# Cross attention's softmax by blocks of 1024 keys instead of by two passes over all keys

## The chip, the cores and the metric

The kernel runs on one core of one Trainium2 chip. The metric is the device time of one execution in microseconds (us), lower is better. Five engines work from queues of their own: TensorE (PE in the profile; PEld are its weight loads), VectorE (DVE), ScalarE (ACT), GpSimd (POOL) and SyncE (SP), which issues most DMAs. Each runs its instructions in the order of its queue, and they wait for each other by semaphores.

## The reference

The whole program is a decoder of six parts over 1024 tokens of width 128 and a context of 6404 rows of width 96. The change is in the second part, single-head cross attention (all in float32):

```python
def _L0_xattn_ref(query, key, value, Wq, bq, Wk, bk, Wv, bv):
    q = jnp.einsum('bqd,dh->bqh', query, Wq) + bq      # query: layernorm of x, 1024 x 128
    k = jnp.einsum('bkd,dh->bkh', key, Wk) + bk        # key and value: ctx_768, 6404 x 96
    v = jnp.einsum('bkd,dh->bkh', value, Wv) + bv
    scores = jnp.einsum('bqh,bkh->bqk', q, k)
    weights = jax.nn.softmax(scores, axis=-1)
    return jnp.einsum('bqk,bkh->bqh', weights, v)      # added to x
```

The kernel never makes k or v. It multiplies the queries by the key weights (`qc`, 97 x 1024: 96 context columns and one for the bias), takes scores as `qc` against the context, sums the context's rows by the weights, and applies the value weights to that sum (`w_v`). A column of ones in the context (`ctx_rows`, 97 columns) gives the softmax's denominator.

## The kernel before

Each engine's queue in a part is written out by hand; what stands behind a wait on an engine waits too. `cross_attention` works in two passes, with PSUM's eight banks of 128 x 512 as its workspace.

The **first pass** goes over 8 tiles of 128 queries, and for each over 7 chunks of 1024 keys (the last has 260). PE makes the scores of a chunk, 128 queries by 1024 keys, with two matmuls of 512 columns (L1001), into one of three pairs of banks; DVE takes the maximum over the keys (L957). The scores are then lost. At every eighth chunk a unit of another piece of work is laid in, the keys of a later part ("film keys"): PE multiplies (L800), ACT rounds to bf16 (`hi`, L819; `mid`, L813), DVE and POOL take the remainders (`rest`, L829; `low`, L844), SP stores. There are 7 units of 1024 keys.

Between the passes the maxima are put into the queries, so that the second pass's scores come out with the maximum subtracted (L1007, L1009, L1065).

The **second pass** goes over 51 tiles of 128 keys (the last has 4). PE makes the scores again, now with keys on the partitions and all 1024 queries as columns (L1033, two matmuls), ACT takes the exponential (L1078, 128 x 1024), and PE sums the context's rows by these weights into two banks (L1018, two matmuls with the 97 context columns as weights). Beside it runs a third piece of work, the convolution kernel of a later state-space part ("s4d"): 16 groups, for each of which DVE makes angles (L546, L632, L634, L635), POOL decays (L653), ACT sines and exponentials (L680, L684), DVE their product (L619), PE a product (L715), and for each two groups ACT copies and PE turns the rows (L692, L727, L699). ACT does a pair of groups as one step: a table load and two sines, a table load and two exponentials.

At the end DVE copies the sum out of PSUM (L967) and PE applies the value weights (L1043), eight small matmuls between DVE's divisions (L971, L972).

Every float32 product of PE is two instructions in the profile; a transpose is one.

## Time and profile before

| | us |
|---|---|
| runs of the kernel before | 1661.75, 1729.4, 1659.3; median 1661.75 |
| the profiled execution: its own time | 1659.78 |
| the profiled execution: its span | 1657.9 |
| cross attention's first pass starts, its second pass ends, in the span | 191.7, 504.0 |
| mean granted clock of TensorE over the span | 0.933 of 2.4 GHz |

The span is the profiled time from the first to the last instruction; the remaining 1.9 us lie around it. Times given as places are counted from the span's start. Matmuls are pipelined: a row's length runs to the modelled end of its last instruction, so the pace of a stream of them is the distance between starts.

### The profile page before, as it was taken

What the parts mean: (1) busy time and instruction counts of PE and PEld (TensorE: products, weight loads), DVE (VectorE), ACT (ScalarE), POOL (GpSimd) and SP (SyncE); (2) the same over time, 40 slices, a digit from 0 to 9 for tenths busy, and PEclk for the clock granted to TensorE, in tenths of its full rate; (3) what the DMA queues carried; (4) which work ended last, traced back from release to release, by engine and by line L of the source; (5) the groups of instructions that cost most, each with busy time, mean ns of one, the idle gap of its engine ahead of it and who ended that gap; (6) DMA issues with size and microseconds to landing.
All of it is one profiled execution on the core that took longest, in us unless ns stands there. A gap on an engine that the chain in (4) does not pass through costs nothing. (4 is left out here: it accounts for less than half of the span.)

```text
span 1657.9 us, 19830 instructions
## 1 busy us (share of the span) xinstructions
PE 1369.8 (83%) x6709; PEld 729.4 (44%) x6763; DVE 1255.7 (76%) x2833; ACT 897.2 (54%) x1424; POOL 678.3 (41%) x466
## 2 busy tenths in 40 slices
PE   6677699999997757889899988989875459999798
PEld 2223344333344434355555555555564323333465
DVE  5999567866515669999999999999878657776433
ACT  4666211457543320687778778877852146666311
POOL 2656111112101034688787878878861120000012
PEclk9799899999997878999999999999987759999899
DMA  6000011000005832000000000000040300000000
GB/s 152 1 0 1 28 58 49 0 1 0 1 0 125 174 103 63 1 1 1 1 1 1 1 1 1 1 1 1 7 152 1 89 1 1 1 1 1 1 0 14
DMA packets 32482, 42.99 MB, mean 26 GB/s; under 512 B 14286, under 2 KB 25644, under 8 KB 30992
## 3 DMA queue, kind: packets, MB, share of 16 engines
q1 hardware_dynamic: 29820, 29.61, 6.2%
q10 hardware_dynamic: 2552, 12.02, 3.5%
q8 instruction: 56, 0.92, 0.2%
q14 instruction: 54, 0.44, 0.1%
HBM read 33.48 MB, written 8.14 MB: 25 GB/s over the span
## 5 line engine op out<-in xcount | busy, mean ns | idle before, releaser
L1631 PE MATMUL psum<-film_ka,film_context_qa 97*128 97x427 bf16 (+3 forms) x896 | 329.8, 368 | 74.3 <-DVE film_stage_kept L1810 29.4
L2033 ACT ACTIVATE film_stage_e<-psum,film_stage_bias 128x512 f32<-128x512 f32 (+1 forms) x416 | 273.9, 668 | 96.9 <-PE psum L1633 87.0
L1810 DVE MAX8 film_stage_kept<-psum 128x8 f32<-128x213 f32 (+1 forms) x960 | 318.5, 377 | 6.6 <-PE psum L1633 6.3
L1633 PE MATMUL psum<-film_kb,film_context_qb 128*128 128x427 bf16 (+2 forms) x843 | 306.4, 364 | 0.0
L1882 POOL TENSOR_TENSOR film_stage_e<-film_stage_e 128x1024 f32<-128x1024 f32 (+1 forms) x91 | 207.1, 2276 | 80.7 <-DVE film_stage_e L1852 60.8
L1852 DVE SCALAR_TENSOR_TENSOR film_stage_e<-psum,film_context_top,film_stage_e 128x512 f32<-128x512 f32 (+1 forms) x325 | 231.8, 719 | 8.4 <-ACT film_stage_e L2033 6.7
L1631 PEld LDWEIGHTS psum<-film_ka,film_context_qa 97*128 97x128 bf16 x896 | 92.1, 103 | 195.3 <-DVE film_stage_kept L1810 86.8
L3235 POOL TENSOR_TENSOR residual<-residual,top_expert_kept 128x1024 f32<-128x1024 f32 x7 | 16.5, 2351 | 294.9 <-DVE top_expert_kept L3192 294.9
L1913 PEld LDWEIGHTS psum<-ctx_rows,film_stage_mean_T 128*128 128x128 f32 (+1 forms) x816 | 121.9, 192 | 30.0 <-issue 3.3
L2998 DVE TENSOR_REDUCE gqa_attend_low<-psum 128x1 f32<-128x128 f32 (+7 forms) x128 | 94.1, 755 | 43.1 <-PE psum L2917 40.7
L1913 PE MATMUL psum<-ctx_rows,film_stage_mean_T 128*128 128x96 f32 (+1 forms) x816 | 119.9, 269 | 1.8
L1872 POOL TENSOR_TENSOR film_stage_e<-film_stage_e,film_stage_keep 128x512 f32<-128x512 f32 (+1 forms) x91 | 102.1, 1122 | 32.7 <-ACT film_stage_keep L2009 32.4
L1885 POOL TENSOR_TENSOR film_stage_mean<-film_stage_e 128x512 f32<-128x512 f32 (+1 forms) x91 | 111.8, 1229 | 7.1
L3035 ACT ACTIVATE gqa_attend_prob<-psum 128x512 f32<-128x512 f32 x192 | 84.9, 486 | 51.4 <-PE psum L2930 50.6
L1018 PE MATMUL psum<-cross_attention_prob,ctx_rows 128*97 128x512 f32 (+1 forms) x204 | 99.7, 612 | 12.4 <-ACT cross_attention_prob L1078 12.4
L342 POOL TENSOR_TENSOR mamba_drive<-mamba_relu,mamba_b_all 128x1024 f32<-128x1024 f32 x32 | 77.2, 2414 | 64.7 <-ACT mamba_b_all L467 34.6
L1633 PEld LDWEIGHTS psum<-film_kb,film_context_qb 128*128 128x128 bf16 x896 | 89.7, 100 | 30.4 <-issue 3.6
L1078 ACT ACTIVATE cross_attention_prob<-psum 128x1024 f32<-128x1024 f32 (+1 forms) x51 | 51.0, 1018 | 87.0 <-PE psum L1033 87.0
L1033 PE MATMUL psum<-oss_attention_qc_shifted,ctx_T 97*128 97x512 f32 (+1 forms) x204 | 97.4, 600 | 0.8 <-ACT oss_attention_qc_shifted L1065 0.8
L957 DVE TENSOR_REDUCE cross_attention_tops<-psum 128x1 f32<-128x1024 f32 (+1 forms) x56 | 61.3, 1109 | 36.6 <-PE psum L1001 36.5
L1001 PE MATMUL psum<-ctx_T,cross_attention_qc 97*128 97x512 f32 (+1 forms) x208 | 87.3, 576 | 0.7 <-issue 0.7
L1897 PE MATMUL psum<-ident,film_stage_mean 128*128 128x128 f32 (+1 forms) x408 | 78.4, 273 | 6.1 <-ACT film_stage_mean_T L1985 5.0
(548 smaller groups left out, 2540.3 us busy)
## 6 DMA issues: line engine op xcount, KB each, us to landing
film_kb<-film_k_rows ACTq DMA_DIRECT2D x4, 1601.0 KB
film_ka<-film_k_rows ACTq DMA_DIRECT2D x3, 1601.0 KB
ctx_T<-in_ctx_T SPq DMA_DIRECT2D x1, 2401.5 KB
gqa_experts_w<-in_L_ffn_W SPq DMA_DIRECT2D x1, 2048.0 KB
film_stage_e<-in_dft_ahead SPq DMA_DIRECT2D x1, 1728.0 KB, 8.7
film_k_rows<-cross_attention_film_hi SPq DMA_DIRECT2D x6, 256.0 KB, 2.0
film_k_rows<-cross_attention_film_mid SPq DMA_DIRECT2D x6, 256.0 KB, 2.0
film_k_rows<-cross_attention_film_low SPq DMA_DIRECT2D x6, 256.0 KB, 2.0
```

The costliest lines, as they stand in the source:

```text
L1018: last = pe.matmul(ps[0:CA, 6 + n, :], ctx[0:rows, k, :], prob[0:rows, k % 3, n * HALF:(n + 1) * HALF], start=k == 0, stop=k == KT - 1)
L1033: last = pe.matmul(ps[0:rows, 2 * (k % 2) + n, :], ctx_T[:, k * P:k * P + rows], qc_shifted[:, n * HALF:(n + 1) * HALF], start=True, stop= ...
L1631: pe.matmul(out, a["qa"][0:ROWS, h, rows], a["ka"][0:ROWS, h, c + b:c + b + cols], start=True, stop=False)
L1633: last = pe.matmul(out, a["qb"][:, h, rows], a["kb"][:, h, c + b:c + b + cols], start=False, stop=True)
L1810: last = dve.max(kept[:, h % 2, PER_PIECE * u + s, :], bank[:, lo:hi])
L1852: dve.scalar_tensor_tensor(out=w, in0=weigh_bank(n, h), scalar=a["top"][:, NH * i + h, TOP - 1:TOP], in1=w, op0=ALU.is_ge, op1=ALU.mult).t ...
L1872: link(pool.tensor_tensor(w[h], w[h], keep[:, k % KEEPS, 0:width], ALU.mult))
L1882: link(pool.tensor_tensor(pairs[:, :, 0, :], pairs[:, :, 0, :], pairs[:, :, 1, :], ALU.add))
L1885: pool.tensor_tensor(out, w[0], w[2], ALU.add).then_inc(mean_ready, 1)
L1913: last = pe.matmul(ps[:, 7, 0:DC], mean_T[0:r, n % 2, b:b + P], ctx[0:r, (c + b) // P, 0:DC], start=c + b == 0, stop=c + b + r == S2)
L2033: act.activation(e[:, n % RING, sub, 0:PIECES[u][1]], ps[:, SEARCH_BANKS + q % WEIGH_BANKS, 0:PIECES[u][1]], ACT.Exp, bias=bias[:, i % 2, ...
L2998: dve.tensor_reduce(low[:, b, i:i + 1], pair(2 * (step % 2), (i + 1) * P), AX, ALU.max, negate=True).then_inc(max_read, 1)
```

## The change

The two passes become one loop over 56 blocks (8 query tiles by 7 chunks of up to 1024 keys), with n as the count of the loop:

- PE makes the scores of block n once (L1092 of the changed kernel), queries on the partitions, from queries of opposite sign. DVE takes the minimum over the block's keys (`shift`), and ACT the exponential against that block's own extreme (L1158).
- PE turns the weights of block n-2 with the identity, 128 keys at a time (`turn`, L1049), into PSUM; ACT copies them to SBUF, 512 columns at a time (`copy_turned`, L1129 and L1132); PE multiplies the turned weights (now the stationary operand, 128 x 128) with the 97 columns of the context (`weighted`, L1062). 408 transposes and 408 products in all.
- The sums of the 7 blocks of a query tile stand side by side in one bank, the first four and then the last three. DVE copies them out (`copy_part`), ACT makes the factors between the blocks' extremes (`scale`), and POOL multiplies and adds them (`bring_together`, four instructions for a tile). At the end PE turns the eight sums and ACT copies them (L1177).
- Scores now have two pairs of banks instead of three; two banks are for turned weights, one for the sums, and one (`side`) for the other two pieces of work.
- The film keys come in 13 units of 512 keys, one a block from n = 1. The s4d work is spread by tables over the blocks from n = 2 to 59. A pair's two sines and two exponentials now stand in two successive blocks.
- SP loads the film mask and the s4d inputs ahead of the value weights; POOL's `memset` of `minus_top` is gone; DVE clears the side bank first.

On PE, in the loop. Before, a stretch of the second pass (L1033 scores, L1018 weighted sums):

```order
L1018 MATMUL psum<-cross_attention_prob,ctx_rows 97x512 x2
L1033 MATMUL psum<-cross_attention_qc_shifted,ctx_T 128x512 x2
L1018 MATMUL psum<-cross_attention_prob,ctx_rows 97x512 x2
L1033 MATMUL psum<-cross_attention_qc_shifted,ctx_T 128x512 x2
L1018 MATMUL psum<-cross_attention_prob,ctx_rows 97x512 x2
```

Now, one block of the loop and the start of the next:

```order
L1049 MATMUL psum<-ident,cross_attention_prob 128x128 x4
L1062 MATMUL psum<-ctx_rows,cross_attention_prob_T 128x97 x4
L1092 MATMUL psum<-ctx_T,cross_attention_qc 128x512 x2
L1049 MATMUL psum<-ident,cross_attention_prob 128x128 x4
L1062 MATMUL psum<-ctx_rows,cross_attention_prob_T 128x97 x4
L735 MATMUL psum<-ident,cross_attention_s4d_rows 128x128 x4
L1049 MATMUL psum<-ident,cross_attention_prob 128x128 x4
```

A block's transposes and products stand in halves around the scores of the block two later; an s4d turn (L735) or product stands at a block's end.

On ACT, around one s4d step. Before, in the second pass:

```order
L692 ACTIVATE cross_attention_s4d_rows<-psum 128x512
L680 ACT_TABLE_LOAD
L680 ACTIVATE cross_attention_s4d_i_angle<-cross_attention_s4d_i_angle 128x1024 x2
L684 ACT_TABLE_LOAD
L684 ACTIVATE cross_attention_s4d_i_decay<-cross_attention_s4d_i_decay 128x1024 x2
L1078 ACTIVATE cross_attention_prob<-psum 128x1024 x2
```

Now:

```order
L1129 ACTIVATE cross_attention_prob_T<-psum 128x512 x2
L1158 ACTIVATE cross_attention_prob<-psum,cross_attention_shift 128x1024
L689 ACT_TABLE_LOAD
L689 ACTIVATE cross_attention_s4d_i_angle<-cross_attention_s4d_i_angle 128x1024 x2
L1129 ACTIVATE cross_attention_prob_T<-psum 128x512 x2
L1158 ACT_TABLE_LOAD
L1158 ACTIVATE cross_attention_prob<-psum,cross_attention_shift 128x1024
L695 ACTIVATE cross_attention_s4d_i_decay<-cross_attention_s4d_i_decay 128x1024 x2
L1129 ACTIVATE cross_attention_prob_T<-psum 128x512 x2
```

Two copies of turned weights now precede each exponential, and the sines (L689) and the decays' exponentials (L695) stand ahead of the copies of the next block.

The core of the diff (the s4d and film functions are cut into steps by index, with the same instructions; the s4d steps are called as shown):

```diff
 def s4d_scalar(act, k, step):
...
-    else:
-        q = 2 * (step - 3)
+    elif step % 2:
+        q = step - 3
         for b in range(2):
             act.wait_ge(sem["i_ready"], q + b + 1)
             angle = k["i_angle"][:, (q + b) % RING_Q]
             act.activation(angle, angle, ACT.Sin, scale=TURN).then_inc(sem["sin_done"], 1)
+    else:
+        q = step - 4
         for b in range(2):
             act.wait_ge(sem["grown"], q + b + 1)
...
+S4D_SMALL_AT = {0: 2, 1: 3, 6: 4, 7: 5, 8: 6, 2: 7, 3: 8, 4: 9, 5: 10, 9: 11, 10: 12}
+S4D_FROM = 12
...
-KEY_PARTS, KEY_RESTS, KEYS_FIRST, KEYS_EVERY = 2, 2, 4, 8
+KEY_UNITS = [(c, min(HALF, S2 - c)) for c in range(0, S2, HALF)]
+KEY_PARTS, KEY_RESTS, KEYS_FIRST = 2, 2, 1
...
+    LAG, PROBS, TURNED = 2, 3, 3
+    FIRST_PART = 4
+    key_at = {KEYS_FIRST + u: u for u in range(len(KEY_UNITS))}
+    small_at = {n: part for part, n in S4D_SMALL_AT.items()}
+    angles_at = {S4D_FROM + 5 * x // 4: divmod(x, 2) for x in range(2 * NG)}
+    pair_at = [S4D_FROM + 5 * p for p in range(NG // 2)]
+    scalar_at = {5: 1, 8: 2}
+    for p, n in enumerate(pair_at):
+        scalar_at[n + 4], scalar_at[n + 5] = 2 * p + 3, 2 * p + 4
+    decay_at = {n + 2 * b: 2 * p + b for p, n in enumerate(pair_at) for b in range(2)}
+    power_at = {n + 6 + b: 2 * p + b for p, n in enumerate(pair_at) for b in range(2)}
+    product_at = {n + 8 + b: 2 * p + b for p, n in enumerate(pair_at) for b in range(2)}
+    rows_at = {n + 10: p for p, n in enumerate(pair_at)}
+    turn_at = {n + 11: p for p, n in enumerate(pair_at)}
+    kernel_at = {n + 12: p for p, n in enumerate(pair_at)}
...
+            def bring_together(i):
+                pool.wait_ge(part_copied, 2 * i + 2)
+                pool.wait_ge(scale_ready, i + 1)
+                x = sums[:, i % 2]
+                link(pool.tensor_tensor(x, x, scale[:, i, :].unsqueeze(2).to_broadcast([P, NB, CA]), ALU.mult))
+                link(pool.tensor_tensor(x[:, 0:3], x[:, 0:3], x[:, 3:6], ALU.add))
+                link(pool.tensor_tensor(x[:, 0:2], x[:, 0:2], x[:, 2:7:4], ALU.add))
+                pool.tensor_tensor(total[:, i, :], x[:, 0], x[:, 1], ALU.add).then_inc(total_ready, 1)
...
         @block.vector
         def _(dve):
...
+            for n in range(END):
+                if n in parts_at:
+                    copy_part(parts_at[n])
+                if n < BLOCKS:
+                    i, c = divmod(n, NB)
                     dve.wait_ge(score_done, n + 1)
+                    dve.tensor_reduce(shift[:, i, c:c + 1], scores(n), AX, ALU.min).then_inc(shift_ready, 1)
...
+                if n in key_at:
+                    film_key_vector(dve, film, side, key_at[n])
+                if n in small_at:
+                    s4d_vector_small(dve, link, s4d, side, small_at[n])
+                if n in angles_at:
+                    s4d_vector_angles(dve, link, s4d, *angles_at[n])
+                if n in power_at:
+                    s4d_vector_power(dve, s4d, power_at[n])
...
         @block.tensor
         def _(pe):
+            def turn(n, h):
+                k = half_at[n, h]
+                pe.wait_ge(prob_ready, n + 1)
+                if k >= 2:
+                    pe.wait_ge(turned, k - 1)
+                for _, x, rows in key_tiles(n, h):
+                    last = pe.transpose(ps[0:rows, 4 + k % 2, x:x + P],
+                                        prob[:, n % PROBS, h * HALF + x:h * HALF + x + rows], g["ident"][:])
+                last.then_inc(turn_done, 1)
+            def weighted(n, h):
+                k = half_at[n, h]
...
+                pe.wait_ge(turned, k + 1)
+                if h == 0 and c in (0, FIRST_PART) and part >= 1:
+                    pe.wait_ge(part_copied, part)
+                for tile, x, rows in key_tiles(n, h):
+                    last = pe.matmul(ps[:, SUMS_BANK, place:place + CA], prob_T[0:rows, k % TURNED, x:x + P],
+                                     ctx[0:rows, tile, :], start=tile % 8 == 0,
+                                     stop=tile == min(8 * c + 7, KT - 1))
...
+            for n in range(END):
+                b = n - LAG
+                if 0 <= b < BLOCKS:
+                    turn(b, 0)
+                if 0 <= b - 1 < BLOCKS:
+                    weighted(*HALVES[half_at[b - 1, 0] + ((b - 1, 1) in half_at)])
+                if n < BLOCKS:
+                    if n >= 2:
+                        pe.wait_ge(prob_ready, n - 1)
...
+                if (b, 1) in half_at:
+                    turn(b, 1)
+                    weighted(b, 0)
+                if n in key_at:
...
+                    film_key_tensor(pe, film, ctx_T, side, key_at[n])
+                if n in product_at:
...
+                    s4d_tensor(pe, s4d, side, product_at[n])
+                if n in turn_at:
+                    s4d_turn(pe, s4d, side, turn_at[n])
...
         @block.scalar
         def _(act):
...
+            for n in range(END):
+                b = n - LAG
+                for h in range(2):
+                    if (b, h) in half_at:
+                        copy_turned(b, h)
+                if n < BLOCKS:
+                    act.wait_ge(shift_ready, n + 1)
+                    act.activation(prob[:, n % PROBS, 0:width(n)], scores(n), ACT.Exp, scale=-1.0,
+                                   bias=shift[:, i, c:c + 1]).then_inc(prob_ready, 1)
...
+                if n in key_at:
+                    film_key_high(act, film, side, key_at[n])
+                if n - 1 in key_at:
+                    film_key_middle(act, film, key_at[n - 1])
+                if n in scalar_at:
+                    s4d_scalar(act, s4d, scalar_at[n])
+                if n in rows_at:
+                    s4d_copy_rows(act, s4d, side, rows_at[n])
+                if n in kernel_at:
+                    s4d_copy_kernel(act, s4d, side, kernel_at[n])
```

## Rows read from the trace of the kernel before

**Rows 1.** Busy time by stretch; columns: stretch, its length, engines, PEclk, DMA

```profile
191.00:290.00 99.00, 96.91 (x234) 44.30 (x234) 68.22 (x64) 15.48 (x17) 13.42 (x7) 1.00 0.14 50
295.00:504.00 209.00, 196.46 (x696) 78.56 (x695) 110.58 (x125) 116.84 (x123) 27.99 (x15) 0.98 0.00 1
```

**Rows 2.** Instructions of two lines of PE: ns min/median/max, first and last start

```profile
L1001 PE MATMUL psum<-ctx_T,cross_attention_qc x208: 381/592/667, 191.7 to 288.3; 97*128 97x512 f32 x96, 97*128 97x260 f32 x8
...
L1018 PE MATMUL psum<-cross_attention_prob,ctx_rows x204: 587/592/1071, 298.3 to 503.3; 128*97 128x512 f32 x100, 4*97 4x512 f32 x2
```

**Rows 3.** Timeline of PE in both passes: start, us to the last end

```profile
255.81 12.62 PE L1001 MATMUL psum<-ctx_T,cross_attention_qc 97*128 97x512 f32 x30
...
376.68 0.62 PE L715 MATMUL psum<-ss_attention_s4d_i_angle,cross_attention_s4d_left 128*8 128x128 f32 x16
377.23 0.66 PE L727 MATMUL psum<-ident,cross_attention_s4d_rows 128*128 128x128 f32 x4
377.73 1.88 PE L1033 MATMUL psum<-oss_attention_qc_shifted,ctx_T 97*128 97x512 f32 x4
```

**Rows 4.** Timeline of PE in causal attention and film context, later parts

```profile
571.34 1.95 PE L1376 MATMUL psum<-causal_attention_v,causal_attention_pT 128*128 128x128 f32 x16
573.13 0.82 PE L1364 MATMUL psum<-ident,causal_attention_score 128*128 128x128 f32 x6
573.78 1.02 PE L1351 MATMUL psum<-causal_attention_kT,causal_attention_qT 128*128 128x512 f32 x2
...
901.36 0.58 PE L1913 MATMUL psum<-ctx_rows,film_stage_mean_T 128*128 128x96 f32 x4
901.78 0.35 PE L1631 MATMUL psum<-film_ka,film_context_qa 97*128 97x426 bf16 x1
```

**Rows 5.** Weight loads of L1376: ns min/median/max, first and last start

```profile
L1376 PEld LDWEIGHTS psum<-causal_attention_v,causal_attention_pT x72: 186/192/192, 571.2 to 589.9; 128*128 128x128 f32 x72
```

**Rows 6.** The stretch of causal attention's stream, columns as in Rows 1

```profile
570.00:580.00 10.00, 8.41 (x61) 7.03 (x60) 6.23 (x15) 4.13 (x8) 0.00 (x0) 1.00 0.42 86
```

**Rows 7.** Timeline of ACT around one s4d step of the second pass

```profile
337.65 1.02 ACT L1078 ACTIVATE cross_attention_prob<-psum 128x1024 f32<-128x1024 f32 x1 [2.41 <-PE psum L1033]
338.69 1.28 ACT L680 ACT_TABLE_LOAD   x1
339.99 2.00 ACT L680 ACTIVATE ss_attention_s4d_i_angle<-ss_attention_s4d_i_angle 128x1024 f32<-128x1024 f32 x2
...
345.21 1.92 ACT L1078 ACTIVATE cross_attention_prob<-psum 128x1024 f32<-128x1024 f32 x2
```

**Rows 8.** PE after that step: timeline, its stretch, and waits in 295 to 504

```profile
342.61 1.88 PE L1033 MATMUL psum<-oss_attention_qc_shifted,ctx_T 97*128 97x512 f32 x4
346.27 3.63 PE L1018 MATMUL psum<-cross_attention_prob,ctx_rows 128*97 128x512 f32 x4 [1.78 <-ACT cross_attention_prob L1078]
...
346.00:350.00 4.00, 3.73 (x5) 1.47 (x6) 3.90 (x4) 1.13 (x2) 2.58 (x1) 0.57 0.02 4
...
PE psum L1018 <- ACT cross_attention_prob L1078: 12.4, 9, 2.8
```

**Rows 9.** Durations on ACT, DVE and POOL: ns min/median/max; the last by form

```profile
L1065 ACT ACTIVATE oss_attention_qc_shifted<-psum x2: 597/597/597, 292.3 to 294.1; 97x512 f32<-97x512 f32 x2
...
L2033 ACT ACTIVATE film_stage_e<-psum,film_stage_bias x416: 459/687/707, 669.6 to 1222.4; 128x512 f32<-128x512 f32 x128, 128x260 f32<-128x260 f32 x11
...
L957 DVE TENSOR_REDUCE cross_attention_tops<-psum x56: 418/1224/1226, 193.8 to 289.4; 128x1 f32<-128x1024 f32 x48, 128x1 f32<-128x260 f32 x8
...
L1885 POOL TENSOR_TENSOR film_stage_mean<-film_stage_e 128x512 f32<-128x512 f32 x84 | 106.7, 1270 | 6.6
```

**Rows 10.** Timeline at the start of cross attention and at its end

```profile
177.55 7.39 DVE L100 TENSOR_SCALAR cross_attention_xn<-residual,cross_attention_mv,cross_attention_rstd 128x128 f32<-128x128 f32 x8
...
179.12 5.67 POOL L836 TENSOR_SCALAR s_attention_film_masking<-ross_attention_film_mask 4x1601 bf16<-4x1601 uint8 x1 [3.49 <-DMA ross_attention_film_mask<-in_vision_mask]
...
505.28 0.71 PE L1043 MATMUL psum<-cross_attention_w_v,cross_attention_summed_c 97*128 97x129 f32 x4 [1.39 <-DVE cross_attention_summed_c L967]
```

More of the change, by code:

```diff
@@ L623, in s4d_vector, with s4d_vector_angles @@
+def s4d_vector_angles(dve, link, k, q, part):
+    sem = k["sem"]
+    b = q % RING_Q
+    group = slice(q * GROUP, (q + 1) * GROUP)
     i_index = k["index"][:, 0:P].unsqueeze(1).to_broadcast([P, GROUP, P])
[L624 to L626 removed]
+    if part == 0:
         if q >= RING_Q:
@@ new lines, in weighted @@
+            def weighted(n, h):
+                k = half_at[n, h]
+                i, c = divmod(n, NB)
+                part = 2 * i + (c >= FIRST_PART)
+                place = (c - part_blocks(part)[0]) * CA
+                pe.wait_ge(turned, k + 1)
[5 more added lines that the diff above has]
+                                     stop=tile == min(8 * c + 7, KT - 1))
+                if (n, h + 1) not in half_at and c in (FIRST_PART - 1, NB - 1):
+                    last.then_inc(part_done, 1)
@@ L1047, in _, with copy_turned @@
         def _(act):
+            def copy_turned(n, h):
+                k = half_at[n, h]
+                act.wait_ge(turn_done, k + 1)
+                whole = sum(rows == P for _, _, rows in key_tiles(n, h)) * P
+                last = act.activation(prob_T[:, k % TURNED, 0:whole], ps[:, 4 + k % 2, 0:whole], ACT.Copy)
+                for _, x, rows in key_tiles(n, h):
+                    if rows < P:
+                        last = act.activation(prob_T[0:rows, k % TURNED, x:x + P], ps[0:rows, 4 + k % 2, x:x + P],
+                                              ACT.Copy)
+                last.then_inc(turned, 1)
             root(act, rstd, 1, var_ready, root_ready)
```

455 lines of the change are left out of this document (213 added, 242 removed).

## The prediction

> **What bounds the kernel now.** I read the busy time by stretch first, because the change lies in cross attention alone. PE is busy for 96.9 of 99 us in the first pass and 196.5 of 209 us in the second, while no other engine passes 117 us [rows 1]. So PE bounds both passes. Then I read places: the scores begin at 191.7 and the last weighted sum starts at 503.3 [rows 2], and the value weights follow at 505.3 [rows 10]. The stretch from 191.7 to 505.3 is 313.6 us; this is what the change replaces. Last I read PE's pace, the distance between starts, since a row's length holds a pipelined end. The question is what PE has to do in the new loop, and whether DVE and ACT, which now stand inside one chain with it, let it do so.
>
> **PE's work, before and after.** 30 score instructions of 512 columns take 12.62 us [rows 3], less the last one's overhang of 0.16, so 0.43 us each; a product is two, 0.86. One 1024-key block of scores costs 1.72. The second making of the scores and the wide sums (each 51 x 2 products, some 88 us at this pace) go. In their place stand 408 transposes and 408 products of 97 columns with fresh 128-column weights. The trace has both kinds in later parts. Six transposes take 573.78 - 573.13 = 0.65 us, 0.11 each; 16 product instructions of 128 columns take 573.13 - 571.34 = 1.79, 0.112 each; four of 96 columns take 0.42, 0.105 each [rows 4]. The nearest bounds are thus 0.105 and 0.112 for a product instruction (I take 0.107, since 97 columns is next to 96) and 0.11 to 0.125 for a transpose, the upper from four s4d transposes between 377.23 and 377.73 [rows 3]; I take 0.11, the longer stream.
>
> - A full block: scores 1.72, 8 transposes 0.88, 16 product instructions 1.71: 4.31 us. 48 of them: 206.9.
> - A 260-key block: scores 2 x 0.22 (half the columns of 0.43), 3 transposes, 6 instructions: 1.40. Eight: 11.2.
> - Film keys, 24 instructions of 512 columns and two of 260: 10.7. The same as before.
> - s4d: 16 products of 0.55 and 8 turns of 0.50 [rows 3]: 12.8. The same as before.
>
> Together 241.6 us against 313.6: a PE that never waited would save 72. The bounds of the two paces move this by -2 to +10.
>
> **What PE waits for in the loop.** A full block on PE runs: turn to 0.44, weighted to 1.30, scores to 3.02, turn to 3.46, weighted to 4.31. A consumer starts some 0.2 us after the pace's end (the overhang). DVE's minimum over 1024 columns takes 1.22 [rows 9] and ends at 4.45. ACT's exponential took 1.02 without a tile as bias [rows 7]; with one, 512 columns take 0.69 where a copy of 512 takes 0.60 [rows 9], so I take 1.11, to 5.6. ACT's two copies are 0.60 each. ACT's load in a plain block is 2.3 of 4.31, and block n's exponential is needed only at 8.6. Plain blocks do not wait. With 1.2 us of film key rounding on ACT and 0.86 on PE they do not either: the next copy ends at 7.4 and is needed at 8.6.
>
> The s4d steps are another matter, since they stand ahead of the copies on ACT. Sines: table load 1.28 and two sines 2.00 [rows 7] push ACT from 5.6 to 8.9, the next copy to 9.5, and PE, which needs the turned weights, can go on at 9.8 (0.3 for the wake and the weight load). Its own work would bring it there at 4.31 + 0.55 (the s4d product) + 3.46 = 8.3. Wait 1.5. Then ACT: second copy 10.1, table load 11.4, exponential 12.5, two decays 14.5 (as long as the sines), rows 15.1, copy 15.7, PE at 16.0. PE itself: weighted 10.7, next turn, weighted, scores, turn, 14.1. Wait 1.9. Then ACT catches up. So 3.4 for a pair of groups, eight pairs: **27.2**. The method can be held against the old kernel: there an ACT step of the same instructions ended with an exponential at 346.2, PE was due at 342.61 + 1.72 = 344.33, and went on at 346.27 [rows 7, 8].
>
> The early s4d steps: at n = 5 two table loads and short functions (2.1 ahead of the copy) overrun by 1.2. At n = 8 a sine over 2048 columns (twice 1.0), two loads and an exponential, 5.6 ahead of the copy: 4.6. DVE's strings of small instructions in n = 2 to 12, up to 3.5 us a block by their columns, delay a minimum by up to 2 and so a copy by about 0.9, three times: 2.7. Together **8.5**.
>
> **The clock.** After the wait of 1.78 us four instructions took 3.63 instead of 1.88, and the granted clock in 346 to 350 was 0.57 [rows 8]: PE fell to 1.2 GHz. The mean of 0.98 over the second pass's 209 us [rows 1] is 8 us at half clock, two such drops for nine waits [rows 8]. For 18 waits now, four drops of 1.75, half of it while ACT catches up: **3.5**.
>
> **Start and end.** The first block's chain (minimum, exponential) leaves PE idle for 0.6, the last blocks 0.6; DVE's copy of the finished sums lands behind angles in some blocks, 1.0 in all. After the last weighted sum before, the value weights waited 505.3 - 503.7 = 1.6 (503.7 is the last start and one pace). Now: overhang 0.2, DVE's copy 0.4, POOL's four instructions, turn 0.3. POOL takes 1.27 for 512 columns [rows 9], 2.5 ns a column with its fixed part: 679 columns 1.7, 291 0.8, 194 0.6, 97 0.4, with links 3.8. Sum 4.7. In the prologue POOL's masking (5.67) held DVE's normalisation, which took 7.39 [rows 10]; the mask now lands some 0.7 us earlier and DVE begins 0.5 later, so fewer tiles escape: **+0.8**, between 0 and 2. What the parts behind do is unchanged.
>
> **The sum.** 241.6 + 0.6 + 0.6 + 27.2 + 8.5 + 1.0 + 3.5 + 4.7 = 287.7 against 313.6, less 0.8: 25.1 us saved. The profiled execution took 1659.8 (1.9 below the median of 1661.75), so **1635 us**.
>
> **Rivals.**
>
> *The waits are absorbed.* The hand schedule spaces the steps, and some fall on short blocks (260 keys), where fewer copies stand in the way. If only a third of 27.2 + 8.5 + 3.5 remains, 26 more is saved: 1609. For it: ACT's mean load leaves a seventh free. Against it: the old kernel's waits came out as reckoned.
>
> *The clock falls after each wait.* 18 drops of 1.75 instead of four halves: 28 more, 1663, no gain. For it: nearly all waits are between 1.5 and 2, like the one that led to a drop. Against: only two of nine did.
>
> *Weight loads come into the open (slower).* A weight load of 128 columns lasts 0.192 [rows 5]; before it was hidden under 0.43 of streaming. Were the 816 product instructions paced by it and not by 0.107, 816 x 0.085 = 69 more: 1704. It turns to a loss from a pace of 0.137. Against it speaks the stream of L1376, same shape of weights, at 0.112. The Trainium skill (TensorE: Matmul & The Clock Gate, Part 3) says that weight loads overlap matmuls in flight only where their row groups differ; here all weights take all 128 rows. By that rule the slower time would come out, but the trace disagrees: 0.192 of loading in a pace of 0.112.
>
> *The transposes keep the clock down.* A fifth of PE's time is now transposes. If the loop ran at 1.2 GHz, PE's 241.6 would double, ACT's waits vanish under it (-40): 1837. Against it: the stretch with the six transposes, a mix like the new one, was granted 1.00 [rows 6]. The same page (Part 4: PE-mode transpose) says that transposes do not count as PE's activity and that the full clock does not come with them; by rows 6 it does in a mix.
>
> **How the numbers follow.** Forecast (save 8 to 42, own range 1618 to 1652): 0.62. Absorbed: 0.17. Clock: 0.12. Weight loads: 0.04. Transposes at half clock: 0.02. A stall that I have not seen: 0.03. The range of 1606 to 1664 takes in the first three cases up to their ends. Two per cent, about what a measurement of this kernel can tell from no change, is 33 us: faster means under 1626.6, which the absorbed case gives and 0.15 of the forecast's: 0.32. Slower, over 1693: 0.07. Same: 0.61.
>
> **What would show it.** Product instructions of L1062 at a pace of 0.105 to 0.112, transposes at 0.11; plain blocks at 4.3 us without idle PE; PE waits of 1 to 2 us on ACT's copies (L1129) behind each sine and decay step, 25 to 40 us in all; some stretches of clock near 0.5; POOL some 3.8 us at the very end. A PE that waits for DVE's minimum or for POOL in plain blocks would show my schedule wrong, and so would weight loads that do not overlap.

## The result, and the profile after

The changed kernel took **1675.69 us** (median of 5 runs, 1671.84 to 1678.91) against 1662.2 in the same session: a ratio of **1.0085, 95% interval 1.0068 to 1.0101**, 14 us slower. I had forecast 1635, with 1606 to 1664 as the range. Both the side and the range were missed. (One of the five runs of the kernel before, 1729.4 us, fell in a slower state of the chip; the ratio is of the others.)

The page of the changed kernel, its first section, and two of the costliest groups (line, busy time and mean ns of one, idle time before them):

```profile
PE 1358.6 (81%) x7566; PEld 812.1 (48%) x7567; DVE 1276.1 (76%) x2860; ACT 959.2 (57%) x1561; POOL 707.2 (42%) x503
...
L1062 PE MATMUL psum<-ctx_rows,cross_attention_prob_T 128*128 128x97 f32 (+1 forms) x816 | 117.0, 288 | 46.9 <-ACT cross_attention_prob_T L1129 26.5
...
L1062 PEld LDWEIGHTS psum<-ctx_rows,cross_attention_prob_T 128*128 128x128 f32 (+1 forms) x816 | 107.8, 205 | 53.6 <-ACT cross_attention_prob_T L1129 33.8
```

The stretch that I had summed, from the first scores (193.80) to the value weights (519.68), lasts 325.9 us. It was 313.6 before [rows 2, 10], and I had reckoned 287.7. So the question is where 38.2 us came from. DVE's minima (L1021) stand one in each of the 56 blocks of 1024 keys and cut the stretch. The start of minimum n=0 is at 195.83, that of n=14 at 296.03, the last at 508.33. Until n=13, DVE also has the film keys' subtractions, and until n=12 the strings of small s4d instructions; the angle strings begin at n=12, and behind 14 come ACT's sine and decay steps for the pairs. My own terms, cut at the same places:

| part | reckoned | after |
|---|---|---|
| first scores to minimum 0 | 2.0 | 2.0 |
| early: minimum 0 to 14 (scores of 1 to 14 21.5, turns and products up to block 11 29.5, film keys 10.3, early s4d 8.5, fill 0.6) | 70.4 | 100.2 |
| late: minimum 14 to 55 (scores 62.8, turns and products 99.1, the last film key 0.4, s4d 11.2, ACT's steps 27.2, copy of sums 1.0, clock 3.5) | 205.2 | 212.3 |
| end: minimum 55 to the value weights | 10.1 | 11.35 |

Of the 38.2 us that were missing, 29.8 lie in the early blocks. The busy time by stretch, early and late (columns: us, busy time and instructions of each engine, granted clock, share of DMA):

```profile
195.83:296.03 100.20, 73.13 (x357) 51.11 (x356) 67.78 (x84) 48.23 (x73) 20.14 (x17) 0.86 0.14 48
...
296.03:508.33 212.30, 190.22 (x1300) 142.12 (x1299) 134.22 (x134) 139.81 (x192) 50.75 (x40) 0.95 0.01 2
```

In the first pass of before PE was busy for 96.9 of 99 us [rows 1]. Now it is idle for 27 of 100, and no engine is full: DVE, the busiest beside it, has 67.8. So I looked for a chain through several of them. What PE waited for between 193 and 296 (us in all, times, longest):

```profile
PE psum L1062 <- DVE cross_attention_sums L1009: 15.9, 2, 10.0
PE psum L1062 <- ACT cross_attention_prob_T L1129: 10.7, 3, 8.5
```

and between 296 and 516:

```profile
PE psum L1062 <- ACT cross_attention_prob_T L1129: 15.8, 13, 2.4
PE psum L1062 <- DVE cross_attention_sums L1009: 3.4, 4, 1.5
PE psum L735 <- ACT cross_attention_s4d_rows L703: 1.9, 1, 1.9
PE psum L1062 <- ACT cross_attention_prob_T L1132: 1.0, 1, 1.0
```

Two waits for DVE's copy of the sums make 15.9 us: a copy that takes half a microsecond. PE's own timeline (start, duration; in brackets the idle time before it) shows a plain block with film keys, and then the first of these waits:

```profile
205.85 0.60 PE L1049 MATMUL psum<-ident,cross_attention_prob 128*128 128x128 f32 x4
206.29 1.03 PE L1062 MATMUL psum<-ctx_rows,cross_attention_prob_T 128*128 128x97 f32 x8
207.16 1.05 PE L807 MATMUL psum<-ctx_T,cross_attention_film_w_k 96*128 96x512 f32 x2
208.05 0.60 PE L1049 MATMUL psum<-ident,cross_attention_prob 128*128 128x128 f32 x4
208.49 1.03 PE L1062 MATMUL psum<-ctx_rows,cross_attention_prob_T 128*128 128x97 f32 x8
209.35 1.91 PE L1092 MATMUL psum<-ctx_T,cross_attention_qc 97*128 97x512 f32 x4
211.10 0.60 PE L1049 MATMUL psum<-ident,cross_attention_prob 128*128 128x128 f32 x4
...
220.31 0.60 PE L1049 MATMUL psum<-ident,cross_attention_prob 128*128 128x128 f32 x4
226.82 1.99 PE L1062 MATMUL psum<-ctx_rows,cross_attention_prob_T 128*128 128x97 f32 x8 [5.90 <-DVE cross_attention_sums L1009]
228.60 1.96 PE L807 MATMUL psum<-ctx_T,cross_attention_film_w_k 96*128 96x512 f32 x2
```

A block with keys takes PE 211.10 - 205.85 = 5.25 us, as reckoned: four transposes in 0.44, eight products in 0.87. PE runs at this pace until 220.9 and then stands still for 5.90. Behind it eight products take 1.99 where they took 1.03: the clock has fallen. What kept DVE? Its timeline over one of the blocks in front:

```profile
206.16 1.22 DVE L1021 TENSOR_REDUCE cross_attention_shift<-psum 128x1 f32<-128x1024 f32 x1
209.05 0.69 DVE L831 TENSOR_TENSOR ross_attention_film_rest<-psum,cross_attention_film_hi 128x512 f32<-128x512 f32 x1 [1.67 <-ACT cross_attention_film_hi L814]
209.66 1.19 DVE L560 TENSOR_SCALAR ross_attention_s4d_angle<-ross_attention_s4d_turns 128x128 f32<-128x128 f32 x1
210.88 0.23 DVE L561 TENSOR_SCALAR ross_attention_s4d_angle<-ross_attention_s4d_turns 128x128 f32<-128x128 f32 x1
...
212.19 0.56 DVE L565 TENSOR_TENSOR ross_attention_s4d_angle<-ross_attention_s4d_angle,ss_attention_s4d_rounded 128x384 f32<-128x384 f32 x1
212.67 1.22 DVE L1021 TENSOR_REDUCE cross_attention_shift<-psum 128x1 f32<-128x1024 f32 x1
```

From minimum to minimum DVE takes 6.51 us, 1.26 more than PE, and the second minimum doesn't wait for PE: it follows the string without a gap. Three pieces make the 6.51. The 1.67 of waiting is a round trip: ACT writes `hi` (L814) only behind the exponential of the same block, and this exponential needs the minimum that DVE has just made. The film subtraction stands next on DVE, and the whole string queues behind it. And the first instruction of the string takes 1.19 us where its neighbour of the same size takes 0.23; POOL's `low` ran at that moment (that the two belong together is shown by the run with small `low` below):

```profile
209.61 1.16 POOL L850 TENSOR_TENSOR cross_attention_film_low<-ross_attention_film_rest,cross_attention_film_mid 128x512 bf16<-128x512 f32 x1 [3.77 <-ACT cross_attention_film_mid L821]
```

The distances between minima 3 to 9 are 6.51, 6.45, 7.47, 9.69, 7.52 and 6.79 us. PE is up to two blocks ahead and doesn't feel it until it needs the copy of the sums (start 226.11), which stands behind a string on the late DVE.

The rest can be put down quickly. In the prologue the first scores come 17.64 us after the start of cross attention and not 17.23 (+0.4, reckoned +0.8). The change makes the stretch 12.3 us longer. The other 6.7 us by which the profiled span grew (1676.9 against 1657.9) are the 0.4, 0.6 in the value products, and parts whose code is the same.

### The profile page after: what moved, and what is told of

Same layout as the page of the kernel before. It is cut to its first block and busy times, and to the rows that moved or that the text cites. A ratio compares the mean times of both kernels' runs of the same rounds, so it can differ in the third digit from the quotient of the medians.

```text
span 1676.9 us, 21828 instructions
## 1 busy us (share of the span) xinstructions
PE 1358.6 (81%) x7566; PEld 812.1 (48%) x7567; DVE 1276.1 (76%) x2860; ACT 959.2 (57%) x1561; POOL 707.2 (42%) x503
## 5 line engine op out<-in xcount | busy, mean ns | idle before, releaser
L1727 PE MATMUL psum<-film_ka,film_context_qa 97*128 97x427 bf16 (+3 forms) x896 | 331.3, 370 | 73.5 <-DVE film_stage_kept L1906 29.5
L1729 PE MATMUL psum<-film_kb,film_context_qb 128*128 128x427 bf16 (+3 forms) x896 | 328.1, 367 | 0.0
L1062 PE MATMUL psum<-ctx_rows,cross_attention_prob_T 128*128 128x97 f32 (+1 forms) x816 | 117.0, 288 | 46.9 <-ACT cross_attention_prob_T L1129 26.5
L1062 PEld LDWEIGHTS psum<-ctx_rows,cross_attention_prob_T 128*128 128x128 f32 (+1 forms) x816 | 107.8, 205 | 53.6 <-ACT cross_attention_prob_T L1129 33.8
L1021 DVE TENSOR_REDUCE cross_attention_shift<-psum 128x1 f32<-128x1024 f32 (+1 forms) x56 | 62.1, 1108 | 81.8 <-PE psum L1092 81.6
L1092 PE MATMUL psum<-ctx_T,cross_attention_qc 97*128 97x512 f32 (+1 forms) x208 | 99.4, 599 | 0.7 <-ACT cross_attention_qc L1147 0.7
L1129 ACT ACTIVATE cross_attention_prob_T<-psum 128x512 f32<-128x512 f32 (+1 forms) x104 | 58.2, 578 | 69.8 <-PE psum L1049 69.4
L1158 ACT ACTIVATE cross_attention_prob<-psum,cross_attention_shift 128x1024 f32<-128x1024 f32 (+1 forms) x56 | 57.4, 1026 | 50.3 <-DVE cross_attention_shift L1021 50.2
```

The source lines that it names most:

```text
L1062: last = pe.matmul(ps[:, SUMS_BANK, place:place + CA], prob_T[0:rows, k % TURNED, x:x + P], ctx[0:rows, tile, :], start=tile % 8 == 0, sto ...
L1092: last = pe.matmul(ps[:, 2 * (n % 2) + h, 0:cols], qc[:, i * P:(i + 1) * P], ctx_T[:, c * CHUNK + h * HALF:c * CHUNK + h * HALF + cols], s ...
L1727: pe.matmul(out, a["qa"][0:ROWS, h, rows], a["ka"][0:ROWS, h, c + b:c + b + cols], start=True, stop=False)
L1729: last = pe.matmul(out, a["qb"][:, h, rows], a["kb"][:, h, c + b:c + b + cols], start=False, stop=True)
```

## The experiments

All edit the changed kernel. Times are medians; the parts are read from the minima of each one's trace. The runs stem from five sessions, in which the median of the kernel before lay between 1661.0 and 1662.2 us; so times of different sessions can be off against each other by about 1 us, and the parts are the better measure. ("Both" means DVE's order and ACT's steps in its gap.)

| | time | ratio to before (95%) | early | late | end |
|---|---|---|---|---|---|
| after | 1675.7 | 1.0085 (1.0068 to 1.0101) | 100.2 | 212.3 | 11.35 |
| DVE's order | 1657.5 | 0.9991 (0.9977 to 1.0005) | 81.9 | 213.4 | 11.35 |
| ACT's steps in its gap | 1660.9 | 1.0002 (0.9991 to 1.0014) | 99.1 | 200.8 | 11.32 |
| both | 1639.1 | 0.9869 (0.9845 to 0.9892) | 75.9 | 202.2 | 11.35 |
| no sine tables | 1651.8 | 0.9951 (0.9935 to 0.9966) | 100.0 | 192.4 | 11.32 |
| after, again | 1676.8 | 1.0091 (1.0070 to 1.0111) | 100.0 | 212.2 | 11.35 |
| small `low` | 1665.5 | 1.0013 (1.0001 to 1.0025) | 90.0 | 212.2 | 11.36 |
| both, three blocks behind | 1642.7 | 0.9889 (0.9868 to 0.9909) | 74.1 | 203.1 | 14.83 |
| both, no sine tables | 1623.0 | 0.9783 (0.9751 to 0.9814) | 75.4 | 187.7 | 11.33 |
| all late strings behind the copy | 1656.0 | 0.9959 (0.9943 to 0.9975) | 76.2 | 218.1 | 11.32 |
| the same, end on DVE | 1654.1 | 0.9954 (0.9941 to 0.9967) | 75.9 | 218.3 | 10.11 |
| some behind, end on DVE | 1636.9 | 0.9862 (0.9841 to 0.9883) | 71.4 | 207.0 | 10.10 |
| both, again | 1637.5 | 0.9853 (0.9837 to 0.9870) | 76.0 | 202.3 | 11.36 |

**DVE's order.** The string that doesn't need `hi` goes ahead of the subtraction that does:

```
-                if n in key_at:
-                    film_key_vector(dve, film, side, key_at[n])
                 if n in small_at:
                     s4d_vector_small(dve, link, s4d, side, small_at[n])
+                if n in key_at:
+                    film_key_vector(dve, film, side, key_at[n])
```

> VectorE's program alone is changed: in each of blocks 1 to 13 of cross attention the string of small state-space operations now stands ahead of the subtraction of the film keys (line 831), not behind it, so that VectorE no longer stands idle for 1.67 us behind the minimum waiting for ScalarE's copy `hi`, which waits for the exponential. Theory 1 (VectorE's round trip, minimum, exponential, hi, subtraction, string, next minimum, sets the pace of blocks 2 to 13: 6.5 to 7.5 us against 5.2 of TensorE's work): 11 x 1.67 = 18 us less, up to 25 with the two long waits for the copy of the sums (5.9 and 10.0 us), so 1651 to 1658 against 1676 of the changed kernel as it is. Theory 2 (the strings are long because GpSimd's operation `low` holds VectorE, 0.95 us a block): the hold stays in the string, less than 5 us. Theory 3 (TensorE's own work at a half clock sets these blocks): less than 5 us.

The time fell by 18.2 us, all of it in the early blocks (18.3). That speaks for theory 1 and rules out theory 3, by which less than 5 should have gone. DVE in the same place now:

```profile
205.85 1.22 DVE L1021 TENSOR_REDUCE cross_attention_shift<-psum 128x1 f32<-128x1024 f32 x1 [1.43 <-PE psum L1092]
207.00 0.22 DVE L560 TENSOR_SCALAR ross_attention_s4d_angle<-ross_attention_s4d_turns 128x128 f32<-128x128 f32 x1
...
208.56 0.56 DVE L565 TENSOR_TENSOR ross_attention_s4d_angle<-ross_attention_s4d_angle,ss_attention_s4d_rounded 128x384 f32<-128x384 f32 x1
209.03 0.68 DVE L831 TENSOR_TENSOR ross_attention_film_rest<-psum,cross_attention_film_hi 128x512 f32<-128x512 f32 x1
211.10 1.22 DVE L1021 TENSOR_REDUCE cross_attention_shift<-psum 128x1 f32<-128x1024 f32 x1 [1.38 <-PE psum L1092]
```

The minimum waits for PE again, and the distance is PE's 5.25. The string fills the time that was a wait. My expectation was wrong in one thing: it said that POOL's hold would stay in the string, but L560 takes 0.22 here. POOL's `low` (209.31 to 210.46) now falls where DVE is idle. So this run alone can't part theory 1 from theory 2: both costs went at once.

**POOL's hold by itself.** `low` is computed on 16 of 512 columns (the rest of it is zeroed once, ahead of the loop):

```
-    pool.tensor_tensor(f["low"][:, u % KEY_PARTS, 0:w], f["rest"][:, u % KEY_RESTS, 0:w],
-                       f["mid"][:, u % KEY_PARTS, 0:w], ALU.subtract).then_inc(sem["low_ready"], 1)
+    pool.tensor_tensor(f["low"][:, u % KEY_PARTS, 0:16], f["rest"][:, u % KEY_RESTS, 0:16],
+                       f["mid"][:, u % KEY_PARTS, 0:16], ALU.subtract).then_inc(sem["low_ready"], 1)
```

> The changed kernel with GpSimd's subtraction `low` (line 850) on 16 of 512 columns, the rest of `low` zero (part of the computation is left out: the low part of the film keys). Its hold on VectorE, some 0.95 us at the head of each string of small operations in blocks 2 to 12, goes. Theory 1 (VectorE's program paces these blocks): every us taken from it counts, 11 x 0.95 = 10 us less, 1663 to 1668. Theory 2 (the hold is the cause of the whole loss in these blocks): over 18 us less. Theory 3 (TensorE's own work): less than 3 us.

The time fell by 11.3 us against the run again beside it, the early part by 10.0. The wait for `hi` is still there:

```profile
208.76 0.69 DVE L831 TENSOR_TENSOR ross_attention_film_rest<-psum,cross_attention_film_hi 128x512 f32<-128x512 f32 x1 [1.67 <-ACT cross_attention_film_hi L814]
209.37 0.25 DVE L560 TENSOR_SCALAR ross_attention_s4d_angle<-ross_attention_s4d_turns 128x128 f32<-128x128 f32 x1
```

As theory 1 says, what is taken from DVE (its busy time in the early blocks went from 67.8 to 56.9 us) comes off the time nearly one for one, and the hold is a part of the loss but not the whole. More than half of the 18.3 us that DVE's order removes can also be had from POOL alone.

**ACT's steps in its gap.** Behind the first copy of turned weights ACT idles, some 2.4 us in a plain block, so the step goes there:

```
                 for h in range(2):
                     if (b, h) in half_at:
                         copy_turned(b, h)
+                    if h == 0 and n in scalar_at:
+                        s4d_scalar(act, s4d, scalar_at[n])
...
-                if n in scalar_at:
-                    s4d_scalar(act, s4d, scalar_at[n])
```

> ScalarE's program alone is changed: each state-space step (sine, decay) moves from behind the exponential to between the two copies of the turned weights of the next stop of the loop, where ScalarE idles some 2.4 us. Theory A (of the late blocks, 14 to 55: these steps stand ahead of the first copy, and TensorE waits for it, 15.8 us in 13 waits, and loses its clock there): 20 to 27 us less, so 1649 to 1656. Rival B (the second copy then comes as late as the first did, or VectorE and GpSimd set the late blocks): less than 5 us either way.

14.8 us less, 11.5 of them in the late blocks. Rival B is out. It is less than theory A's 20, since part of the wait stays: 9.1 us in 12 waits for L1129, and 6.5 in 7 for the copy of the sums, where 3.4 in 4 had been.

**No sine tables.** The sine activation of the pair steps (L689) becomes an exponential:

```
-            act.activation(angle, angle, ACT.Sin, scale=TURN).then_inc(sem["sin_done"], 1)
+            act.activation(angle, angle, ACT.Exp, scale=TURN).then_inc(sem["sin_done"], 1)
```

> The sine of the pair steps is replaced by an exponential of the same size (part of the computation is changed: sines and cosines are not computed), so that ScalarE loads no other function table in these steps. Prices the table loads. Theory A (ScalarE's steps ahead of the copies hold TensorE): a step with 1.3 us a load and two loads a pair becomes short enough to hide, 15 to 25 us less, 1651 to 1661. Rival B: less than 5 us.

23.9 us less, 19.9 of them in the late blocks (the stretch explains 20.2; the other 3.7 lie outside it and between sessions): more than moving the steps gave, and near the upper end. The sixteen loads at 1.28 us are 20.5 us of ACT's time. The late blocks' gain is of about that size, but it isn't the loads' time passed on: PE's idle time there fell by 11.0 us (22.1 to 11.1), and its busy time by 8.9 (190.2 to 181.3), because the granted clock was 0.99 and not 0.95.

**Both moves.**

> Both moves at once. If both theories hold, the gains lie in different blocks (2 to 13 and 14 to 55) and add: 38 to 52 us less, 1624 to 1638, which would be faster than the kernel before the change (1662). If the early blocks are set by something else (theories 2, 3), it comes out as the move on ScalarE alone does.

36.6 us less than the changed kernel, just short of the 38 that I had expected at least: the two gains (18.2 and 14.8) add, and some. In the early blocks there are 6.0 more than with DVE's order alone. This is block 9 to 10, 13.56 us in the changed kernel, 13.20 with DVE's order, 11.06 with ACT's and 7.00 with both. ACT's timeline there in the changed kernel:

```profile
246.07 0.59 ACT L814 ACTIVATE cross_attention_film_hi<-psum 128x512 bf16<-128x512 f32 x1
246.54 0.63 ACT L821 ACTIVATE cross_attention_film_mid<-ross_attention_film_rest 128x512 bf16<-128x512 f32 x1
247.19 1.28 ACT L682 ACT_TABLE_LOAD   x1
248.49 1.91 ACT L682 ACTIVATE ss_attention_s4d_j_angle<-ss_attention_s4d_j_angle 128x2048 f32<-128x2048 f32 x1
250.41 1.28 ACT L683 ACT_TABLE_LOAD   x1
251.71 1.06 ACT L683 ACTIVATE ss_attention_s4d_j_decay<-ss_attention_s4d_j_decay 128x1024 f32<-128x1024 f32 x1
252.67 1.07 ACT L1129 ACTIVATE cross_attention_prob_T<-psum 128x512 f32<-128x512 f32 x2
253.63 1.12 ACT L1158 ACTIVATE cross_attention_prob<-psum,cross_attention_shift 128x1024 f32<-128x1024 f32 x1
```

A step of 5.5 us stands ahead of two copies and an exponential. PE waited 8.48 us for the copy. With DVE's order alone the same step made PE wait 4.63:

```profile
242.49 2.02 PE L1062 MATMUL psum<-ctx_rows,cross_attention_prob_T 128*128 128x97 f32 x8 [4.63 <-ACT cross_attention_prob_T L1129]
```

and with both moves this wait is gone. Both queues had to be mended for this block.

**Both, and no sine tables.**

> Both moves, and the sine of the pair steps replaced by an exponential (part of the computation is changed: sines and cosines are not computed), so that 16 table loads go. Tells what the table loads still cost when the steps stand in ScalarE's gaps. If the gap hides them wholly: 1636 to 1640, as both moves alone. If the late blocks still pay for the loads: 8 to 12 us less, 1627 to 1631.

16.1 us less than both moves, where I had expected 12 at most (the stretch explains 15.1 of them). The run with both moves shows why the gap hid so little:

```profile
305.90 1.28 ACT L689 ACT_TABLE_LOAD   x1
...
309.52 0.60 ACT L1129 ACTIVATE cross_attention_prob_T<-psum 128x512 f32<-128x512 f32 x1 [0.32 <-PE psum L1049]
310.14 1.28 ACT L1160 ACT_TABLE_LOAD   x1
```

Only the sine's load stands between the two copies, and with it the step lasts 3.3 us where the gap is some 2.4. The load that brings the exponential's table back stands behind the second copy, ahead of the exponential: eight of the sixteen loads never were in the gap. Of the 14.5 us by which the late blocks are shorter here, 7.4 are idle time of PE and 7.1 its clock (0.97 with both moves). This run also shows what the late blocks cost almost without waits for ACT (1.3 us in three). The stretch from minimum 14 to 55 (the columns as before):

```profile
268.39:456.07 187.68, 179.29 (x1300) 134.60 (x1299) 138.23 (x135) 118.81 (x176) 54.91 (x40) 1.00 0.01 2
```

The same 1300 PE instructions are busy for 179.3 us at a clock of 1.00, and were for 190.2 at 0.95. So of the 24.6 us between this run and the changed kernel, 10.9 are clock and 13.7 are idle time of PE.

**Three blocks behind.** LAG, PROBS = 3, 4 in place of 2, 3.

> Both moves of the run before, and the turning of the weights three blocks behind the scores and not two, with four buffers of weights and not three. If TensorE waits for ScalarE because exponential, turning and copy of neighbouring blocks follow each other too closely, 5 to 10 us less than both moves alone (1639), so 1629 to 1634. If what is left are waits for the copy of the turned weights and for the copy of the sums, which keep their places beside each other on their engines, within 4 us of it: 1635 to 1643.

3.6 us more than both moves, near the upper bound of the second case (the intervals of the two overlap; the stretch is 2.5 longer). Early and late together are 1.0 us shorter, and the one more block that is left at the end costs 3.5. More distance between exponential and turning isn't what was lacking.

**The changed kernel again.**

> The changed kernel again, with nothing altered: what the same program gives beside the others on this chip, and whether the 3.9 us by which its unchanged part behind cross attention was longer in its first profile (1150.4 against 1146.5) come back. If they belong to the one profiled execution: that part at 1145 to 1147, the time 1672 to 1679. If the change causes them: 1150 again.

The parts repeat within 0.2 us, the time within 1.1. The part behind the stretch took 1148.2 us here and 1150.4 at first, by the same code. In the other profiled executions it lay between 1142 and 1148, so a few us between two spans belong to that part and not to the edit. My expectation named 1145 to 1147 or 1150, and it was neither.

**Late strings behind the copy.** With both moves PE still waited 13.9 us in 10 waits for the copy of the sums. A string that stood ahead of the copy goes behind it and the minimum that follows:

```
+                if n - 1 in held:
+                    strings(n - 1)
+                if n not in held:
+                    strings(n)
```

(held: the blocks from 14 on that stand before a copy; strings: the small instructions, film subtraction, angles and products of a block.)

> Both moves, and from block 14 on VectorE's string of state-space operations that stands ahead of a copy of the sums (line 1009) moves behind the copy and the minimum that follows it. In the run with both moves TensorE waited 13.9 us in 10 waits for this copy. If VectorE's order alone causes these waits, those of the late blocks go: 6 to 10 us less than both moves alone (1639), so 1629 to 1633. If the strings are then late for ScalarE, whose steps now stand between the two copies of turned weights, the wait comes back there: 1637 to 1645.

> The same, and the last of the eight bringings together (multiply and three additions, 3.0 us on GpSimd, for which TensorE waits 2.5 us at the end) on VectorE instead of GpSimd. VectorE took 0.42 to 1.23 us for operations on 128x260 to 128x1024 values; four of 679, 291, 194 and 97 columns come to 1.6 to 2.2 us with their starts. So 0.8 to 1.4 us less than the run without it, within what five rounds can just tell.

17 us slower than both moves, worse than the rival I had written. What PE waited for in the run with both moves, over the whole stretch:

```profile
PE psum L1062 <- DVE cross_attention_sums L1009: 13.9, 10, 4.4
PE psum L1062 <- ACT cross_attention_prob_T L1129: 9.1, 12, 1.5
```

and now:

```profile
PE psum L1069 <- ACT cross_attention_prob_T L1136: 21.7, 13, 3.7
PE psum L1069 <- DVE cross_attention_sums L1009: 7.4, 3, 4.4
```

The late waits for the copy went (6.5 us in 7 before, all of these 7.4 are early), and the late ones for ACT more than doubled (9.1 to 21.3). ACT itself waited for DVE's angles (L689 for L640) for 0.3 us in one wait with both moves, and now:

```profile
ACT ss_attention_s4d_i_angle L689 <- DVE ss_attention_s4d_i_angle L640: 7.8, 5, 4.2
```

So some sine steps are late, stand between two copies, and hold PE. This is a part of it at most, and how large a part isn't shown. Another cause lies beside it in the trace and wasn't tested: behind a held string two strings stand ahead of the next minimum, and ACT's waits for DVE's minimum went from 24.0 us, longest 2.9, to 28.3, longest 4.9. And of the 15.9 us by which the late blocks grew, only 6.2 are idle time of PE; 9.7 are its clock, 0.92 where it was 0.97. The second kernel's end went from 11.32 to 10.11: DVE does the last four operations 1.2 us sooner than POOL.

**Only the strings that ScalarE doesn't wait for.**

```
+                if n - 1 in angles_at and n - 1 in late_angles:
+                    s4d_vector_angles(dve, link, s4d, *angles_at[n - 1])
+                if n - 1 in power_at and n - 1 in held:
+                    s4d_vector_power(dve, s4d, power_at[n - 1])
                 strings(n)
```

(late_angles: the held blocks whose angle string isn't the last of its pair. Here `held` takes in the early blocks too, so the first angle string, at n=12, also goes behind its copy.)

> As the run with the last bringing together on VectorE, but only those strings stand behind the copy of the sums and its minimum whose result ScalarE's next step doesn't wait for: the products (L649 in the trace) and the first three of the four angle strings of a pair. If the loss of the run before (13 waits for ScalarE, 21.7 us, against 9.1) came from ScalarE's sine step waiting for a string that had been put back: 1630 to 1634, under both moves alone by the 6.5 us of waits for the copy that went, and 1 us of the tail. If any string put behind a minimum costs as much as it gives: 1638 to 1650.

> Both moves alone once more, beside the run before on the same chip, in more rounds: 1636 to 1641, ratio to the kernel before 0.985 to 0.990.

1636.9 against 1637.5: between my two cases, and no difference from both moves that the intervals can tell. The early part is 4.6 us shorter (the block from 12 to 13 went from 8.53 to 4.60, and PE's wait of 4.4 for the copy there to 0.5), but the late part is 4.7 longer, and only the 1.2 us of the end stay. ACT still waited 4.5 us for angles in 2 waits, and PE 17.8 for ACT's copies. So the waits for angles (4.2 us more than with both moves) explain at most half of PE's 8.7 us more for the copies, and the cause of the rest stays open. In the late blocks, moving work behind the copy on DVE traded one wait for another; in the early ones it paid. Which other order would avoid both wasn't tried. The best kernel of the study is thus the one with both moves, 1.3 to 1.5% faster than the kernel before.

## Why the prediction was wrong

**PE's work: right.** Products of 97 columns came at 0.109 (8 in 0.87) where I took 0.107, transposes at 0.11, a block with keys at 5.25 against 4.31 + 0.86. Both slow rivals about PE are out. (One reading was loose: the 30 score instructions of rows 3 can't all have 512 columns, since 30 at 0.43 would take 12.9. With two of 260 among them they take 28 x 0.43 + 2 x 0.22 = 12.5, as shown, so the pace of 0.43 stands.) A weight load lasts 192 ns in the median, and a load and a product together pass every 0.109, so the two overlap. This is against the rule of the Trainium skill (TensorE: Matmul & The Clock Gate, Part 3) that only loads for other row groups overlap. The loads may not be free even so: at the scores' pace 97 columns would take 0.081. What makes it 0.109 no run shows. And a block in which 8 of 30 instructions are transposes was granted 1.00 (205.85 to 211.10).

**The step that failed** was: "With 1.2 us of film key rounding on ACT and 0.86 on PE they do not either: the next copy ends at 7.4 and is needed at 8.6." I followed PE and ACT through such a block, and not DVE. I had durations for it: minimum 1.22, exponential 1.11, `hi` 0.6, subtraction some 0.7, a string of up to 3.5. As measured in DVE's order they are 1.22 + 1.67 + 0.61 + 3.0 = 6.5, over PE's 5.25. About 0.95 of the 3.0 is POOL's hold, which I couldn't have had from columns; but without it the block still takes 5.57 (the run with small `low`) and the five behind it 5.5 to 7.3. "DVE's strings ... delay a minimum by up to 2 and so a copy by about 0.9, three times: 2.7" treated each string as a delay that passes. But DVE had no slack to win it back with: from minimum 3 to 14 all eleven blocks took longer than PE's 5.25, and it added up. The early part took 29.8 us more than I had put in. DVE's order alone takes 18.3 of it away, ACT's steps in the gap alone 1.1, both 24.3; and the first angle string behind its copy takes 4.6 more, which brings the early part to 71.4, against the 70.4 that I had reckoned. The run with small `low` shows that about 10 us of it is POOL's hold, which I had left out: I priced strings by their columns. Before the change this loop hadn't bound, since PE was busy for 96.9 of 99 us there [rows 1]; that its blocks were longer than DVE's trip is inferred from this, not tested.

**The other place for DVE's lateness:** "DVE's copy of the finished sums lands behind angles in some blocks, 1.0 in all". Two such waits alone cost 15.9 us. They are how the lateness reaches PE. In the late blocks the same term was 3.4.

**ACT's steps, 27.2: mechanism right, size fair.** The late waits for ACT are 15.8 + 1.9 + 1.0 = 18.7 us in 15 waits, the longest 2.4. That is a third under the sum. The signs that I had named (waits of 1 to 2 us on L1129, 25 to 40 in all) came out at 26.5, 10.7 of them early. The step at n = 8, put at 4.6, made a wait of 8.48, because the minimum's lateness stood on top of it: with DVE's order mended the wait was 4.63.

**The clock, 3.5: too small.** The late part alone lost 10.9 us of PE's busy time to it, and 5.8 in the early one (73.1 busy against 67.4 with both moves, at 0.86 and 0.96). The rival of 1663 had the clock as its cause, and would have been nearer in number; it had nothing on DVE's loop.

**The end and the prologue** were right within 1.2 and 0.4 us. POOL's four operations took 516.29 to 519.51, 3.2 against 3.8.

With the failed step mended by an edit of two lines, and ACT's steps moved, the kernel takes 1639 and 1637.5 us, near the forecast of 1635: not because the forecast was right. Its sum left out what DVE's order removes, and it held more for ACT's steps (27.2) and less for the clock (3.5) than the runs show; that these nearly cancel is luck. (The sum was also taken from the profiled execution's 1659.8; from the median of 1662.2 in the result's session it gives 1637. And its two per cent as what a measurement can tell was far too wide: the ratio was known to 0.2%.)

## What to carry to other kernels

When a change shortens the block on the engine that bounds, walk every engine's program through one block in its own order, with its waits for others' answers, and compare the walk with the new block. Mean busy time (DVE had 68 of 100 us) doesn't show such a loop (the distance between the same instruction in neighbouring blocks does, 6.5 us on DVE against 5.25 on PE), and PE's waits name only the place where lateness is collected. If a queue must wait for an answer to its own last result, put the work that doesn't need the answer between the two.

## What the runs showed that I had not expected

- A DVE multiplication, addition or rounding (TENSOR_TENSOR, TENSOR_SCALAR, SCALAR_TENSOR_TENSOR) that read SBUF alone and began while POOL ran lasted longer by about what POOL had left. With POOL's 128x512 subtraction (1.16 us) just begun this was some 0.95 us, whatever the DVE instruction's size (0.23 became 1.19, and one over 1024 columns 2.19 instead of 1.22); one that began 1.7 us before the end of a POOL instruction of 2.88 us took 2.80 instead of 1.23. Instructions that read PSUM weren't lengthened: in the run with DVE's order L831 at 220.00 took 0.69 and the copy at 220.60 took 0.55, with `low` running from 219.80 to 220.98. Nor was a reciprocal (0.95 inside and outside of a POOL instruction), nor one that had begun before POOL: L831 at 209.03 took 0.68 with `low` starting at 209.31. Where DVE was idle anyway, the hold cost nothing.
- A pair of groups has two function table loads, and only one of them moved into ACT's idle time with the sine step; the one ahead of the exponential stayed. Taking out all sixteen, 1.28 us each, still gave back 16.1 us then, and 23.9 in the changed kernel; in the late blocks about half of either was PE's clock.
- After 5.90 us of idle time PE ran at half pace for several microseconds, with the granted clock at 0.50 from 226.8 to 231 and at 0.72 between 224 and 236. In the late blocks, where no wait was longer than 2.4 us, the mean was 0.95.
